# Order of the weight loads, transposes and evictions at the start of a gated cross-attention and mixture-of-experts kernel

## The reference

```python
q = (layernorm(x) @ Wq); k = context @ Wk * SCALE; v = context @ Wv     # 16 heads of 64
attn = softmax(q k^T); out = attn v @ Wo + bo
x = x + tanh(g_xattn) * out
x = x + tanh(g_ffn) * moe(layernorm(x))       # 8 experts, top 2 for each batch, 256 -> 1024 -> 256
```

## Time and profile before

| what | value |
| --- | --- |
| median of 3 runs | 328.48 us (328.46 to 330.07) |
| the profiled execution's own time | 328.43 us |
| its span on the chip | 326.6 us |
| PE busy | 315.9 us, 97% of the span |
| DVE, ACT, POOL busy | 230.7, 165.9 and 83.0 us |
| mean granted clock of TensorE | 0.998 |

### The profile page before, as it was taken

One profiled execution on the slowest core, in us unless ns is written; L12 is line 12 of the kernel. 1 busy time (PEld: TensorE's weight loads), 2 busy tenths in 40 slices (PEclk: granted clock), 3 DMA queues, 4 the chain that ended last, 5 costly groups with the idle time before them and its releaser, 6 DMA issues.

```text
span 326.6 us, 5754 instructions
## 1 busy us (share of the span) xinstructions
PE 315.9 (97%) x1810; PEld 269.4 (83%) x1810; DVE 230.7 (71%) x540; ACT 165.9 (51%) x580; POOL 83.0 (25%) x170
## 2 busy tenths in 40 slices
PE   6999999999999999999899999999999999999993
PEld 6987897989989899887688888888888888888882
DVE  0688889898799989999688675375664753643642
ACT  2548755676776656775366254355542543213220
POOL 1525546574355437327710000000000000000000
PEclk9999999999999999999999999999999999999999
DMA  7991000000000017700007070000000000210001
GB/s 255 385 154 5 1 2 0 2 1 2 1 0 3 0 16 251 252 1 0 0 2 259 4 254 1 0 0 0 2 1 0 0 0 0 85 46 0 34 32 64
DMA packets 20222, 17.26 MB, mean 53 GB/s; under 512 B 10981, under 2 KB 16230, under 8 KB 20070
## 3 DMA queue, kind: packets, MB, share of 16 engines
q1 hardware_dynamic: 19920, 16.44, 16.6%
q10 hardware_dynamic: 278, 0.53, 0.6%
HBM read 14.86 MB, written 2.10 MB: 52 GB/s over the span
## 4 chain that ended last, share of the span: by engine, by line
PE 78%; DVE 9%; ACT 5%; POOL 3%; issue 2%; DMA 2%; DVEq 0%; SPq 0%; POOLq 0%; ACTq 0%
PE ps L1027 23%; PE ps L1029 22%; PE ps L1028 22%; ACT sx L542 4%; PE ps L1129 2%; PE ps L1048 2%; DVE mx L808 2%; DVE pT_lo L772 2%; DMA wk_sb<-in_L_xattn_Wk_dram 2%; PE ps L1095 1%; DVE sm L783 1%; PE ps L1212 1%; PE ps L1268 1%; ACT pT_hi L554 1%; PE ps L1153 1%
## 5 line engine op out<-in xcount | busy, mean ns | idle before, releaser
L632 ACT ACTIVATE gel<-ps,b1sel 128x512 f32<-128x512 f32 x64 | 43.9, 690 | 93.0 <-PE ps L1029 93.0
L992 DVE CAST h_hi<-gel 128x512 fp32r<-128x512 f32 x64 | 27.5, 429 | 58.8 <-ACT gel L632 58.0
L542 ACT ACTIVATE sx<-ps,mx 128x64 f32<-128x64 f32 x128 | 38.2, 328 | 27.7 <-DVE mx L808 27.7
L1027 PE MATMUL ps<-h_hi,w_hi 128*128 128x512 f32 x128 | 50.9, 397 | 0.0
L1027 PE MATMUL ps<-yT_hi,w_hi 128*128 128x512 f32 (+1 forms) x128 | 50.4, 394 | 0.2 <-ACT sx L542 0.2
L1029 PE MATMUL ps<-h_hi,w_lo 128*128 128x512 f32 x128 | 49.9, 390 | 0.0
L1029 PE MATMUL ps<-yT_hi,w_lo 128*128 128x512 f32 (+1 forms) x128 | 49.9, 390 | 0.0
L1028 PE MATMUL ps<-yT_lo,w_hi 128*128 128x512 f32 (+1 forms) x128 | 49.9, 390 | 0.0
L1028 PE MATMUL ps<-h_lo,w_hi 128*128 128x512 f32 x128 | 49.9, 390 | 0.0
L994 DVE TENSOR_TENSOR h_lo<-gel,h_hi 128x512 fp32r<-128x512 f32 x64 | 44.3, 692 | 2.2
L423 POOL TENSOR_TENSOR sx<-sx,rs 128x1024 f32<-128x1024 f32 x16 | 30.5, 1907 | 48.6 <-DVE rs L788 48.0
(11 more groups left out here) (132 smaller groups left out, 606.7 us busy)
## 6 DMA issues: line engine op xcount, KB each, us to landing
stage_w<-in_L_ffn_w_dram SPq DMA_DIRECT2D x7, 1024.0 KB, 7.4
out_dram<-xt SPq DMA_DIRECT2D x8, 256.0 KB, 2.5
xt<-in_x_dram SPq DMA_DIRECT2D x2, 512.0 KB, 8.6
wq_sb<-in_L_xattn_Wq_dram SPq DMA_DIRECT2D x2, 512.0 KB, 7.7
wv_sb<-in_L_xattn_Wv_dram SPq DMA_DIRECT2D x1, 1024.0 KB, 10.1
wo_sb<-in_L_xattn_Wo_dram SPq DMA_DIRECT2D x1, 1024.0 KB, 12.8
xt<-in_x_dram SPq DMA_DIRECT2D x1, 1024.0 KB, 16.1
stage_w<-in_L_ffn_w_dram SPq DMA_DIRECT2D x2, 512.0 KB, 4.7
```

Of the source, the lines that this page charges most:

```text
L542: last = nc.scalar.activation(sx[:, par, c0:c0 + M], ps[:, 2 * par + 1, c0 - BANK:c0 - BANK + M], ACT.Exp, bias=mx[:, par, h:h + 1], accum ...
L632: nc.scalar.activation(gel[:, f % 4, :], ps[:, h_bank, :], ACT.Gelu, bias=b1sel[:, b, slot, f:f + 1]).then_inc(gelu_done, 1)
L992: nc.vector.tensor_copy(h_hi[:, f % 4, :], gel[:, f % 4, :]).then_inc(hhi_ready, 1)
L1027: mm(acc, hi_w, hi_x, start=start, stop=False)
```

## The change

Loads: ACT's queue now carries Wq rows 0 to 127, columns 0 to 511 (256 KB), in place of the second half of Wk. SP issues ctx, the other quarter of the first columns of Wq, Wk's first half, x tiles 0 and 1, Wk's second half, x tiles 2 and 3, the last two quarters of Wq, and then Wv and the rest as before.

PE: the extra warm-up goes; wqT 0 and 1 are transposed right behind ctxT, by quarters (`wq_pair`), then kT 0, kT 1 and the gates' matmul; wqT 2 and 3 stand between score pairs 2 and 4. The banks are dealt anew.

Evictions: all four wqT and both kT are read by ACT, in the order wqT 0, wqT 1, tanh, kT 0, kT 1, A 0 to 3, wqT 2, wqT 3, A 4 to 6. DVE no longer reads kT 1 or wqT 3, and runs all Newton steps of x tiles 0 to 3 itself. POOL zeroes the warm-up tile first, and only waits for DVE's result.

```diff
-        setup_groups = [("ctxT", 0), ("kT", 0), ("kT", 1)] + [("wqT", i) for i in range(4)]
-        groups = setup_groups + A0 + V0 + late_groups
+        WQ0, WQ1 = [("wqT", 0), ("wqT", 1)], [("wqT", 2), ("wqT", 3)]
+        groups = [("ctxT", 0)] + WQ0 + [("kT", 0), ("kT", 1)] + A0[:4] + WQ1 + A0[4:] + V0 + late_groups
-        GRP_BANK = dict(zip(groups, [0, 1, 2, 3, 4, 5, 6, 0, 1, 2, 3, 4, 5, 6, 1, 2, 3, 4, 5, 0, 6] + [0, 1] * len(LATE)))
+        GRP_BANK = dict(zip(groups, [0, 1, 2, 3, 4, 5, 6, 0, 1, 2, 3, 4, 2, 3, 5, 6, 2, 4, 5, 0, 6] + [0, 1] * len(LATE)))
-        ACT_READS = [("kT", 0), ("wqT", 0), ("wqT", 1), ("wqT", 2), ("vT", 0)]
+        ACT_READS = WQ0 + [("kT", 0), ("kT", 1)] + WQ1 + [("vT", 0)]
...
-            sp.dma_start(wk_sb[:, :, 0:HD // 2], Wk.rearrange("(k p) n -> p k n", p=P)[:, :, 0:HD // 2]).then_inc(ld_wk[0], 16)
-            load_x(0, 0, 0, TB // 2)
+            sp.dma_start(wq_sb[:, 1, 0:HD // 2], Wq[P:2 * P, 0:HD // 2]).then_inc(ld_wq[1], 16)
             for half in range(2):
                 cols = slice(half * HD // 2, (half + 1) * HD // 2)
-                sp.dma_start(wq_sb[:, :, cols], Wq.rearrange("(k p) n -> p k n", p=P)[:, :, cols]).then_inc(ld_wq[half], 16)
+                sp.dma_start(wk_sb[:, :, cols], Wk.rearrange("(k p) n -> p k n", p=P)[:, :, cols]).then_inc(ld_wk[half], 16)
+                load_x(3 * half, 0, half * TB // 4, (half + 1) * TB // 4)
+            for k in range(KD):
+                sp.dma_start(wq_sb[:, k, HD // 2:HD], Wq[k * P:(k + 1) * P, HD // 2:HD]).then_inc(ld_wq[2 + k], 16)
...
-            newton(*X_PARTS[0], rstd1, ve_x, 1)
+            pool.wait_ge(guess_ready, 1)
...
-            act.dma_start(wk_sb[:, :, HD // 2:HD], Wk.rearrange("(k p) n -> p k n", p=P)[:, :, HD // 2:HD]).then_inc(ld_wk[1], 16)
+            act.dma_start(wq_sb[:, 0, 0:HD // 2], Wq[0:P, 0:HD // 2]).then_inc(ld_wq[0], 16)
...
+            for g in WQ0:
+                group(*g)
+            act.wait_ge(ld_g, 32)
+            nc.scalar.activation(tg_row[:, :], gg[:, :], ACT.Tanh).then_inc(tanh_done, 1)
             group("kT", 0)
-            for i in range(3):
-                group("wqT", i)
-            for g in A0[:7]:
+            group("kT", 1)
+            for g in A0[:4] + WQ1 + A0[4:7]:
                 group(*g)
...
-                norm(t0, t1, mean1, rstd1, ve_x, (0,))
+                norm(t0, t1, mean1, rstd1, ve_x, range(4) if i == 0 else (0,))
...
+            def wq_pair(half):
+                pair = WQ0 if half == 0 else WQ1
+                for g in pair:
+                    if GRP_BEFORE[g]:
+                        wait_group_read(pe, *GRP_BEFORE[g])
+                for k in range(KD):
+                    pe.wait_ge(ld_wq[2 * half + k], 16)
+                    for g in pair:
+                        for m in range(2):
+                            c0 = (2 * g[1] + m) * P
+                            last = nc.tensor.transpose(ps[:, GRP_BANK[g], (m * KD + k) * P:(m * KD + k + 1) * P],
                                                        wq_sb[:, k, c0:c0 + P], ident[:, :])
+                        if k == KD - 1:
+                            last.then_inc(grp_done, 1)
...
             warm_up(8)
             group("ctxT", 0)
-            warm_up(1)
+            wq_pair(0)
             group("kT", 0)
             group("kT", 1)
             pe.wait_ge(rows_ready, 1)
             pe.wait_ge(tanh_done, 1)
             mm(ps[:, 7, 0:2], ones_row[:, :], tg_row[:, :], start=True, stop=True).then_inc(tg_spread, 1)
-            for i in range(4):
-                group("wqT", i)
-            for i in range(0, 8, 2):
-                score_pair(i)
+            score_pair(0)
+            score_pair(2)
+            wq_pair(1)
+            score_pair(4)
+            score_pair(6)
```

More of the change, by code:

```diff
@@ L165, in gated_cross_attention_moe_kernel @@
         ld_ctx, ld_wv, ld_wo = (sem("ld_" + n) for n in ("ctx", "wv", "wo"))
-        ld_wq = [sem(f"ld_wq_{i}") for i in range(2)]
+        ld_wq = [sem(f"ld_wq_{i}") for i in range(4)]
         ld_wk = [sem(f"ld_wk_{i}") for i in range(2)]
-        ld_x = [sem(f"ld_x_{i}") for i in range(3)]
+        ld_x = [sem(f"ld_x_{i}") for i in range(4)]
         ld_g, ld_bo, ld_gate, ld_b12 = sem("ld_g"), sem("ld_bo"), sem("ld_gate"), sem("ld_b12")
@@ L377, in _ @@
         def _(pool):
+            nc.gpsimd.memset(warm_w[:, :], 0.0).then_inc(warm_ready, 1)
             nc.gpsimd.memset(ident[:, :], 0.0).then_inc(zeros_ready, 1)
@@ L492, in _ @@
             nc.scalar.activation(warm[:, 0:1], ones_row[:, 0:1], ACT.Exp)
-            act.wait_ge(ld_g, 32)
-            nc.scalar.activation(tg_row[:, :], gg[:, :], ACT.Tanh).then_inc(tanh_done, 1)
             def group(kind, i):
@@ L711, in group @@
                     nc.vector.tensor_copy(ctxT[:, :, :], bank[:, 0:D].rearrange("p (k i) -> p k i", k=KD)).then_inc(grp_dve, 1)
[L712 to L719, removed]
                 if kind == "vT":
@@ L741, in x_low @@
                                         ALU.subtract).then_inc(xlo_ready, 1)
-            nc.vector.memset(warm_w[:, :], 0.0).then_inc(warm_ready, 1)
             dve.sem_inc(hlo_ready, FREE_GELS)
             group("ctxT", 0)
-            x_stats(0, range(0, TB // 2))
+            x_stats(0, range(0, TB // 4))
+            x_stats(3, range(TB // 4, TB // 2))
             x_norm(0)
-            group("kT", 1)
             dve.wait_ge(tg_spread, 1)
             nc.vector.tensor_copy(tg[:, :], ps[:, 7, 0:2]).then_inc(tg_ready, 1)
-            group("wqT", 3)
             for g in A0[:6]:
@@ L1049, in group @@
                                       start=(k == 0), stop=(k == KD - 1))
[L1050 to L1055, removed]
+                last.then_inc(grp_done, 1)
[10 more added lines that the diff above has]
+                            last = nc.tensor.transpose(ps[:, GRP_BANK[g], (m * KD + k) * P:(m * KD + k + 1) * P],
                                                        wq_sb[:, k, c0:c0 + P], ident[:, :])
-                last.then_inc(grp_done, 1)
+                        if k == KD - 1:
+                            last.then_inc(grp_done, 1)
             def two_banks(kind, i):
```

## The result

| what | before | changed |
| --- | --- | --- |
| median (20 runs each) | 328.56 us | 329.96 us |
| ratio to before | | 1.0032, 95% interval 1.0017 to 1.0046 |
| the profiled execution's own time, its span | 328.43, 326.6 us | 329.53, 327.7 us |
| start of the first x transposes in it | 16.90 | 18.14 |

The change costs 0.3% by the ratio and its interval; the medians are 1.4 us apart, 0.43%. It is less than half a per cent and so "no change" in the sense of the forecast, but with this many runs the loss is real. The forecast was 329.0 us, with 328.7 to 329.7 as the forecast proper and 327.8 to 330.2 as the range: the median lies outside the first and inside the second. The kernel before has two groups of times, 12 of its 20 runs at 328.4 to 328.6 and 8 at 329.9 or more, so a ratio that weighs all runs comes out smaller than that of the medians.

A forecast was written before the change was run, and what follows sets the result against it. PE, busy for 97% of the span, was taken to bound the kernel. Terms -0.95 + 0.4 + 1.5 - 0.39 = +0.56 us on 328.43 us gave 329.0 us, with a range of 327.8 to 330.2.

The forecast's parts named there:

- The mark: Start of the first x transposes, 16.90 before; whatever moves it was claimed to move the end by as much.
- +0.56: Sum of the forecast's terms for the setup, in us: -0.95 + 0.4 + 1.5 - 0.39.
- wqT 0 and 1 in the old gap: Eight transposes move into PE's idle wait for Wk's first half, ending at 6.63; term -0.95 us.
- the three gaps: PE's idle times in the setup: the wait for Wk's first half, one before the last score pair, the ninth warm-up.
- From the gates' matmul on: PE's walk from the gates' matmul at 10.8 through the score pairs to the x transposes at 17.4.
- The gap: New PE wait before score pair 4, for wqT 2 and 3 evicted by ACT behind A 0 to 3; +1.5 us.
- The pair's old wait: PE's wait before the last score pair for DVE's `a_lo` of A 1; claimed to go, term -0.39 us.
- the room that was claimed: DVE's margin over a microsecond despite the Newton steps; `xn` of tile 0 ready at 14.6, asked for at 17.4.
- kT 1, +0.4: kT 1 waits for Wk's second half, now SP's fifth load, and starts at 8.95; +0.4 us, bounds 0 and 0.7.
- Wk's second half is later: Rival: 256 KB transfers pay for themselves in the queue, 2.1 us on top of the forecast, 331.1 us; 9%.
- The wait at pair 4 isn't there: Rival: ACT keeps up with its evictions, so PE does not wait there; sum -0.9, 327.5 us; 8%.
- PE's clock: Rival: PE falls to 1.2 GHz in the new order, the 32 kT instructions cost 3 us, 332 us; 4%.

The follow-up runs named there:

- changed again: The changed kernel run once more, unedited, on another chip as the reference: 330.28 us, ratio 1.0038 to the kernel before.
- loads alone: The kernel before with only the new order of loads; PE's order, evictions and Newton steps as before: 330.65 us against 328.46, ratio 1.0084.
- kT 1 first: The kernel before with kT 1 ahead of kT 0 on TensorE, nothing else: 327.70 us against 328.46, ratio 0.9975.
- short queue: The kernel before with Wk's second half cut by rows, one quarter on ScalarE's queue, the other on SyncE's: 328.26 us, ratio 0.9989.
- both repairs: The changed kernel with Wk's second half back on ScalarE's queue and wqT 2 and 3 ahead of the score pairs: 329.64 us, ratio 1.0035.
- wqT early: The changed kernel with wqT 2 and 3 transposed and evicted ahead of the score pairs: 329.65 us, ratio 1.0018 to the kernel before.

## Why the prediction was right

**The mark counts one for one.** Here is the own time of each profiled execution less its mark, for seven of the fourteen profiles: before 311.53, changed 311.39, changed again 311.46, loads alone 311.46, kT 1 first 311.39, short queue 311.50, both repairs 311.37; with the mark anywhere from 16.11 to 22.07, thirteen of fourteen profiles lie between 311.3 and 311.6. The exception is the kernel with Newton steps on GpSimd, 311.93, whose time outside the span is the longer one. This step is shown. Nothing behind the setup gave anything back.

**How right.** The range held, and the direction, but the size was off: the median rose by 1.4 us and the mark by 1.24, where +0.56 was forecast. The next profile of the same kernel had kT 1 at 10.79, which the prediction itself had named as a sign that it is wrong (after 9.7), and its mark had moved by 2.5 us. The median of that second set of runs, 330.28 us, lies just above the range. So the account of the waits held and one term did not, and that the total still fell in the range is in part luck: that term was 1.07 us in one profile and 2.4 in the other.

**wqT 0 and 1 in the old gap.** Right: they run from 5.0 to 6.1, and kT 0 starts 0.2 us later than it did, for its load. What could be regained at best was added up wrongly, though: the three gaps of 1.51, 0.39 and 0.39 us are 2.3 us, and its 1.9 takes in only two of them. Nothing in the forecast hangs on it.

**From the gates' matmul on.** Forecast 6.6 us (10.8 to 17.4), measured 6.68 (11.46 to 18.14); before it was 6.51. The gap was forecast at 1.5 us and is 1.5 on the weight loads' side, 1.3 on the matmuls'. ScalarE's chain has the forecast form: `a_hi` from 12.96, wqT from 14.89, 1.93 us for four evictions. The pair's old wait is gone, and DVE, POOL and `xn` had the room that was claimed. That the gap is ScalarE's chain is shown by the kernels with wqT early, which have none.

**The term that was off is "kT 1, +0.4".** The gates' matmul came at 11.46 instead of 10.8, so the term is +1.07: 0.20 for Wk's first half, which I had left at 6.6, 0.73 for the second (from 8.75 to 9.48), and the rest at the matmuls' ends. With 1.07 in place of 0.4 the sum of +0.56 becomes +1.23, and the mark moved by 1.24. I had interpolated landings by bytes at the old order's rate, with 0 to 0.2 us for another transfer, and put the upper bound at 0.7. The rate is not a constant of the stage: it was lower in all seven profiles with the new order. In the changed kernel's second profile the same term is 2.4 us (gates' matmul at 12.77), and in the kernel with the new loads alone it is the whole loss, 1.9 us at the mark.

**The rivals.** The one that came nearest is "Wk's second half is later". Of its price of 2.1 us on top of the forecast, the first profile shows 0.67 and the second 2.0. Its mechanism isn't what the runs show: one more transfer, by a cut of Wk's second half in the kernel before, cost nothing (328.26 and 328.19 us against 328.42), and in the slow profiles the stream as a whole was slower. A price for the cuts of x and Wq was not tried by itself. The 2.1 us was also a weak base: ctx is not a lone transfer, since ScalarE's queue issues its first load at the same 0.73, and the same load of ctx took 2.4 us in the second profile of before and 3.9 in that of the changed kernel. And the page "DMA: Bandwidth & Descriptors" of the Trainium skill, in the section on the anatomy of one DMA that the prediction names, gives its 2.0 us from a fit to transfers issued from GpSimd, while all of these are issued from SyncE and ScalarE. "The wait at pair 4 isn't there" is out. "PE's clock", which I gave 4%, was not in the changed kernel's two profiles, but showed in those of four of the seven variants that keep its new order of loads or a form of it. The balance of the change is then: the loss is in the new loads. The rest of it is near nothing, +0.17 by the profiles (6.68 against 6.51 us from the gates' matmul to the mark, with the transposes that moved already counted). The medians have the loads alone at 2.2 us over before and the whole change at 1.4 and 1.7, but on different chips, and the loads vary by more than that.

**Open.** Why the new order is slower between 4 and 9 us. A short ScalarE queue alone does not do it, nor do the pieces alone: with all of them, and Wk's second half on ScalarE's queue, the rate was 358 and 348 GB/s. What is left is that queue and pieces do it together, and no run takes that apart. What the two pairs of quarters of Wq do together with x in halves was not tried by itself, nor was the changed kernel run with x in one load.

## What to carry to other kernels

When a load is moved in a queue at the start of a kernel, expect the rate itself to change, not only the places: bound the landing with the worst rate seen in the stage, profile the kernel more than once, and check every load that is waited for, also those that "stay". Before reordering loads, look whether the consumer can be reordered: here swapping two groups on TensorE, so that it takes first what lands first, gave 0.25%, while no rearrangement of the queues tried here gave a gain clear of the noise, and all kernels with the new order had medians above before. And when work is inserted into a chain of evictions on one engine, count what stands in front of it there, since the gap of 1.5 us could be read from one row of before.

## What the runs showed of the hardware

**The loads of the first 9 us.** From 4 to 9 us the same loads came at 357 to 381 GB/s in the old order (three profiles) and at 251 to 323 in the new (seven profiles). In single microseconds the DMA engines' share was down to 0.43, at 131 GB/s, with several loads issued and not landed ("wqT early", 4 to 5 us). What held them isn't shown.

**TensorE's clock.** In four variants the granted clock fell from 1.00 to 0.50 behind idle stretches of 1.64, 2.25, 2.44 and 3.19 us in a setup that had already had other gaps; behind 2.21 us of idleness in the last kernel it did not. And the profile's granted clock does not always show the level: the kernel before cut in two pieces has this row, at a granted clock of 1.00 throughout,

```profile
6.44 5.67 PE L1049 MATMUL ps<-ctxT,wk_sb 128*128 128x128 f32 x32 [0.76 <-DMA wk_sb<-in_L_xattn_Wk_dram]
12.04 0.38 PE L1113 MATMUL ps<-tg_row,ones_row 1*128 1x2 f32 x2
```

5.67 us for what takes 3.84 in the earlier trace rows, with some 7 instructions started in each microsecond at first, as in the warm-ups, where the kernel before starts 12. The windows from 7 to 8 us of this kernel and of the kernel before:

```profile
7.00:8.00 1.00, 1.00 (x7) 1.00 1.01 374
```

```profile
7.00:8.00 1.00, 1.00 (x12) 1.00 0.95 363
```

By that spacing TensorE was at its 1.2 GHz level though the profile's granted clock is 1.00, as it also is for the warm-ups. That is the 1.8 us by which this execution exceeds the kernel's median, and near the distance of some 1.6 us between the two groups of times of the kernel before. The same cause is likely, but not shown: no profile of before caught it.
